# A four-layer attention and expert kernel: TensorE's slots regrouped, the sort cut in three, indirect writes paced anew

## The chip, the cores and the metric

The kernel runs on one core of a Trainium2 chip (trn2). The metric is the device time of one execution in microseconds, lower is better. The kernel before took 880.13 us (median of three runs, 880.06 to 884.29).

## What is computed

The input x has 8 sequences of 256 tokens with 128 channels. Four layers follow one another, each on a normalised x and added to it:

```python
x = x + attn_a(layernorm(x))   # "rope": 16 heads of 8 channels, rotated q, k, v, softmax, rotated back
x = x + ffn(layernorm(x))      # "ffn": h = x + attention(ln1(x)); h + experts(ln2(h))
x = x + attn_b(layernorm(x))   # "cov": centred q, k, plus a product of their variances, softmax
x = x + ffn(layernorm(x))
```

The experts of an ffn layer: every token picks the 2 best of 8 by a gate, each expert is gelu(t @ w1 + b1) @ w2 + b2 with 512 hidden channels, and the two results are mixed with normalised gate weights. All arithmetic is float32 (matrix products of the projections and scores use a float32 form that is split into a rounded and a remaining part).

## The kernel before

**Phases.** There are two phases (`ph`), each with two attention layers (rope and ffn, then cov and ffn) and one expert stage (`mixture`). Every engine has its own instruction stream, written out by hand with semaphores (`need`, `wait_ge`, `then_inc`).

**Attention as a pipeline.** A step s works on up to six blocks (a block is one sequence of 256 tokens) at different stages, named u, t, a, m, n, p from oldest to youngest. In each engine's `step(u, t, a, m, n, p)`, p is normalised (`norm`, GpSimd), n is turned, projected and its q and k stacked and turned (`do_zT`, `do_proj`, `do_kT`, `do_qT`), m has its raw scores taken for the maxima (`do_raw` on TensorE, `do_max` on VectorE), a has its scores, exponentials and products with the values (`do_scores`, `do_exp` on ScalarE, `do_pv`), t is divided, turned and projected out (`do_outT`, `divide`, `do_onT`, `do_wo`, `residual`), and u goes through second normalisation and router (`close` on GpSimd, `do_uT`, `do_gate`, `choose`, `weigh`). There are 16 blocks in a phase, so 16 steps in which `a` exists; a step begins here with the first scores of its `a`.

**TensorE's step (lines 591 to 678).** It has eight slots. Each begins with the scores and raw scores of two heads (32 rows of the array an instruction, lines 444 and 457), goes on to some full-array work (128 by 128), and ends with one `do_pv`: four products of 32 columns each, side by side (line 471), for one key half `kc` of a group `g` of four heads. The two key halves of a group are in slots that follow one another.

**Banks.** PSUM gives four banks to what ScalarE reads (`ring_e`), three to what VectorE reads (`ring_r`: raw scores, projections, outT, gate, wo, rank), one to the products. A bank is taken in order of use, and its next writer waits for the reader of its last content.

**Sort and indirect writes.** In the step with a = block 6 of an ffn layer (`ranking`), the first half's tokens are ranked by expert (`do_rank` on TensorE, `sort_rows` on VectorE, lines 1267 to 1304). `scatter` (line 1554) then issues 16 indirect DMAs on GpSimd's queue that write the rows of U to their sorted places, paced by waits for exponentials (first half) or evacuated expert tiles (second half: `PACE_AT`). A half's sorted rows are loaded only after its 16 writes have landed (`load_x` on SP's queue, line 382).

**Expert stage.** 23 tiles of 128 sorted rows a half: `turn_x`, `hidden`, `outputs` on TensorE (lines 702, 714, 727), gelu on ScalarE, `evacuate` on VectorE (line 1319), then stores, gathers and `combine`. `mixture` begins with the last products of the last block and with `do_weT`, whose copy on ScalarE is a line-833 instruction of WT.

**GpSimd's step (lines 1619 to 1644).** In the order: norm(p) if `early`, close(u), stack_k(n), unrope(t), stack_q(n), stack_v(n), and norm(p) last if not early.

## Time and profile before

| | |
|---|---|
| median of three runs | 880.13 us |
| the profiled execution | 881.32 us |
| its span, first to last instruction | 879.5 us |
| TensorE busy | 780.0 us, 89% |
| VectorE / ScalarE / GpSimd busy | 540.4 / 543.9 / 482.8 us |
| mean granted TensorE clock | 0.926 of full |
| L1114, maxima of raw scores (VectorE) | 326.1 us, 512 instructions |
| L839, exponentials (ScalarE) | 277.0 us, 512 instructions |
| L471, products with the values (TensorE) | 175.8 us, 2048 instructions |

Times are microseconds from the start of the span. PE is TensorE, DVE VectorE, ACT ScalarE, POOL GpSimd. "x8" behind a row is eight instructions merged; the first two numbers are the start and the length of the merged run, which includes the drain of its last instruction, so that the next start tells better how long it held the engine. A bracket is the idle time before and what ended it. PEclk is the granted clock as a share of 2.4 GHz; 0.5 is the lower of the two levels.

### The profile page before, as it was taken

What the parts mean: (1) busy time and instruction counts of PE and PEld (TensorE: products, weight loads), DVE (VectorE), ACT (ScalarE), POOL (GpSimd) and SP (SyncE); (2) the same over time, 40 slices, a digit from 0 to 9 for tenths busy, and PEclk for the clock granted to TensorE, in tenths of its full rate; (3) what the DMA queues carried; (4) which work ended last, traced back from release to release, by engine and by line L of the source; (5) the groups of instructions that cost most, each with busy time, mean ns of one, the idle gap of its engine ahead of it and who ended that gap; (6) DMA issues with size and microseconds to landing.
All of it is one profiled execution on the core that took longest, in us unless ns stands there. A gap on an engine that the chain in (4) does not pass through costs nothing.

```text
span 879.5 us, 21305 instructions
## 1 busy us (share of the span) xinstructions
PE 780.0 (89%) x7166; PEld 552.7 (63%) x7166; DVE 540.4 (61%) x1370; ACT 543.9 (62%) x1264; POOL 482.8 (55%) x906
## 2 busy tenths in 40 slices
PE   1999999999999989987988999999999998998970
PEld 1755655656555459986964555666665544897960
DVE  4699998788878423112486888888887852221232
ACT  0377776877776527544556766787786652764630
POOL 6667777747672550514745765734776344142436
PEclk9999998999998759999999999999999975899995
DMA  9400000000000325765310000000000023465842
GB/s 272 119 3 3 3 3 1 3 3 2 3 3 2 101 70 143 203 182 164 88 37 13 18 17 5 4 2 3 2 3 2 3 63 96 119 199 174 239 118 69
DMA packets 57657, 56.29 MB, mean 64 GB/s; under 512 B 6856, under 2 KB 42448, under 8 KB 57552
## 3 DMA queue, kind: packets, MB, share of 16 engines
q1 hardware_dynamic: 39200, 39.13, 15.8%
q0 software_dynamic: 4096, 8.40, 3.2%
q10 hardware_dynamic: 14256, 7.41, 2.9%
q8 instruction: 61, 1.00, 0.5%
q14 instruction: 44, 0.36, 0.1%
HBM read 40.10 MB, written 14.29 MB: 62 GB/s over the span
## 4 chain that ended last, share of the span: by engine, by line
PE 56%; DVE 22%; POOL 7%; issue 6%; DMA 4%; another core or an unknown queue 2%; ACT 2%; ACTq 0%; POOLq 0%; SPq 0%; DVEq 0%
DVE M L1114 11%; PE bankO L471 10%; PE bankE L714 8%; PE bankR L727 7%; PE bankE L490 7%; PE bankE L444 7%; PE bankR L457 3%; POOL Yg L1590 3%; PE bankE L481 2%; PE bankR L511 2%; DVE QKV L1076 2%; DMA Yg<-sorted_y,SLOT 1%; PE bankE L551 1%; PE bankE L702 1%
## 5 line engine op out<-in xcount | busy, mean ns | idle before, releaser
L1114 DVE TENSOR_REDUCE M<-bankR 128x2 f32<-128x512 f32 x512 | 326.1, 683 | 78.1 <-PE bankR L457 75.1
L839 ACT ACTIVATE Pr<-bankE 128x512 f32<-128x512 f32 x512 | 277.0, 594 | 130.9 <-PE bankE L444 123.0
L457 PE MATMUL bankR<-KQ 32*128 32x256 f32 x1024 | 175.7, 341 | 8.3 <-DVE M L1114 4.8
L471 PE MATMUL bankO<-Pr,Vx 128*32 128x256 f32 x2048 | 175.8, 418 | 0.0
L444 PEld LDWEIGHTS bankE<-KQ 32*128 32x128 f32 x1024 | 82.1, 195 | 102.6 <-issue 73.4
L444 PE MATMUL bankE<-KQ 32*128 32x256 f32 x1024 | 136.8, 344 | 0.0
L457 PEld LDWEIGHTS bankR<-KQ 32*128 32x128 f32 x1024 | 113.1, 192 | 22.0 <-DVE M L1114 17.3
L1572 POOL DMA_INDIRECT sorted_u<-U,SLOT x64 | 62.3, 973 | 100.0 <-DVE Yb L1319 58.0
L956 ACT ACTIVATE G<-bankE,W 128x128 f32<-128x128 f32 x368 | 101.0, 381 | 25.6 <-PE bankE L714 14.6
L1319 DVE COPY Yb<-bankR 128x128 f32<-128x128 f32 x92 | 26.1, 289 | 145.3 <-PE bankR L727 126.0
L714 PE MATMUL bankE<-XTT,W 128*128 128x128 f32 x736 | 102.1, 285 | 4.4 <-ACT G L956 1.4
L1590 POOL DMA_INDIRECT Yg<-sorted_y,SLOT x64 | 62.0, 969 | 73.7 <-DMA sorted_y<-Yb 31.2
L727 PE MATMUL bankR<-w,G 128*128 x736 | 98.1, 278 | 2.3 <-DVE Yb L1319 1.9
L714 PEld LDWEIGHTS bankE<-XTT,W 128*128 128x128 f32 x736 | 93.0, 199 | 7.8 <-issue 4.2
L727 PEld LDWEIGHTS bankR<-w,G 128*128 128x128 f32 x736 | 89.4, 192 | 4.1 <-issue 3.2
L833 ACT ACTIVATE KQ<-bankE 128x512 fp32r<-128x512 f32 x128 | 70.5, 604 | 23.4 <-PE bankE L490 22.9
L471 PEld LDWEIGHTS bankO<-Pr,Vx 128*32 128x32 f32 x2048 | 42.0, 112 | 36.2 <-issue 14.3
L1481 POOL CAST Kst<-QKV 128x512 fp32r<-128x512 f32 x24 | 15.7, 653 | 65.4 <-DVE QKV L1076 39.2
L1406 POOL TENSOR_SCALAR lnsmall<-meanvar 128x2 f32<-128x2 f32 x48 | 11.1, 230 | 70.2 <-DVE meanvar L1044 67.3
L490 PE MATMUL bankE<-ident_r,Zhl 128*128 128x256 f32 (+1 forms) x128 | 24.1, 315 | 23.0 <-POOL X L1452 13.4
L947 ACT ACTIVATE XTT<-bankE,lncols 128x512 f32<-128x512 f32 (+1 forms) x24 | 18.3, 763 | 41.6 <-PE bankE L702 41.6
L490 PE MATMUL bankE<-ident_r,Kst 128*128 128x256 f32 (+1 forms) x256 | 39.2, 299 | 4.1 <-POOL Kst L1484 4.1
(169 smaller groups left out, 1147.7 us busy)
## 6 DMA issues: line engine op xcount, KB each, us to landing
W<-in_w1b SPq DMA_DIRECT2D x92, 258.0 KB
sorted_y<-Yb ACTq DMA_DIRECT2D x92, 64.0 KB
XT<-sorted_u SPq DMA_DIRECT2D x20, 256.0 KB
sorted_u<-Yg SPq DMA_DIRECT2D x2, 1472.0 KB, 9.6
KQ<-MT SPq DMA_DIRECT2D x128, 4.0 KB
X<-in_x SPq DMA_DIRECT2D x8, 128.0 KB, 7.7
sorted_u<-U,SLOT POOLq DMA_INDIRECT x64
Yg<-sorted_y,SLOT POOLq DMA_INDIRECT x64
```

Source lines behind the costliest of these rows:

```text
L444: k = mm(act_bank("S", layer, b, h)[:, z * T:z * T + T], KT[rows, kb, g, z * P:z * P + P], QT[rows, kb, g, :], start=True, stop=True)
L457: k = mm(dve_bank("raw", layer, b, h)[:, z * T:z * T + T], QT[rows, kb, g, z * P:z * P + P], KT[rows, kb, g, :], start=True, stop=True)
L471: k = mm(bankO[SL * j:SL * j + SL, cols], Vx[:, b % VB, kc, HG * g + j, :], Pr[:, g % 2, j, kc, :], start=(g % 2 == 0 and kc == 0), stop=( ...
L490: return mm(bank[:, i * P:i * P + n], src, ident_r[:, 0:n], start=True, stop=True)
L714: k = mm(act_bank("hid", ph, at)[:, c * P:c * P + P], W1[:, n % NW, c * P:c * P + P], XTT[:, (ph * NGRP + q) % 2, j, :], start=True, stop= ...
L727: k = mm(dve_bank("out", ph, at)[:, 0:D], G[:, (ph * NAT + at) % NGB, c, :], w2[:, bass.ds(e * FC + c, 1), :].rearrange("p o d -> p (o d)" ...
L833: return nc.scalar.activation(dst, src, ACT.Copy)
L839: nc.scalar.activation(Pr[:, (h // HG) % 2, h % HG], act_bank("S", layer, b, h).rearrange("p (k q) -> p k q", k=TT), ACT.Exp, scale=EXP_SC ...
L956: nc.scalar.activation(G[:, n % NGB, c, :], act_bank("hid", ph, at)[:, c * P:c * P + P], ACT.Gelu_apprx_tanh, bias=W1[:, n % NW, FF + c:FF ...
L1114: v.tensor_reduce(M[:, b % 2, :, h], dve_bank("raw", layer, b, h).rearrange("p (t k) -> p t k", t=TT), AX.X, ALU.max, negate=True).then_in ...
L1572: g.indirect_dma_start(sorted_u[half][:, :], bass.IndirectOffsetOnAxis(ap=SLOT[:, half, n:n + 1], axis=0), U[:, b, t, :], None).then_inc(s ...
L1590: g.indirect_dma_start(Yg[:, n % NYG], None, sorted_y[half][:, :], bass.IndirectOffsetOnAxis(ap=SLOT[:, half, at:at + 1], axis=0)).then_in ...
```

## The change

TensorE's step keeps its eight slots. Both key halves of a group of heads now stand behind one another in every second slot, and all full-array work stands in the slots between. The next block's `do_zT` moves, for rope and ffn layers, to the end of the step before; it waits for one GpSimd instruction less. `do_kT` stands in the sixth slot and `do_qT` in the eighth for all layers; `do_uT` and the second part of `do_rank` move from the third to the fourth slot, `do_gate` from the fifth to the sixth. ScalarE and VectorE follow the new order. GpSimd normalises p first in every step whose p belongs to a rope or ffn layer. `sort_rows` becomes three functions, called in three places of the step. `do_gate` and `choose` on VectorE move behind the norm statistics of the next block. The first half's indirect writes wait at numbers 3, 9 and 12 only, six instead of five are issued in the sort's step, and the second half's wait for tiles two earlier.

```diff
--- before.py
+++ after.py
@@ -248,6 +248,7 @@
         ffn_only = {"ffn": 1}
         ln_stats = event("ln_stats", 4)
         z_ready = event("z_ready", {"rope": 9, "ffn": 15, "cov": 8})
+        Z_READY = {"rope": 8, "ffn": 14, "cov": 8}
         zT = event("zT", 1)
         zT_copied = event("zT_copied", 1)
         proj = event("proj", 2)
@@ -323,7 +324,8 @@
         STEPS = 2 * NB + 5
         FILL, DRAIN = 3, 2
-        EARLY, PACE_AT = 5, 7
+        EARLY, PACE_AT = 6, 5
+        PACE = {3: (NB - 2, 14), 9: (NB - 1, 10), 12: (NB - 1, 16)}
         def block_of(u):
@@ -341,6 +343,10 @@
             q = max(q for q, (first, _) in enumerate(GROUP) if first <= at)
             return q, at - GROUP[q][0]
+        def turned_ahead(q):
+            return LAYERS[q[0]] != "cov"
         def own_steps(ph):
@@ -490,7 +496,7 @@
                 return mm(bank[:, i * P:i * P + n], src, ident_r[:, 0:n], start=True, stop=True)
             def do_zT(layer, b):
-                need(pe, z_ready, layer, b)
+                need(pe, z_ready, layer, b, Z_READY[LAYERS[layer]])
                 ring_e.take(pe, ("zT", layer, b))
                 for x in range(2):
                     for t in range(TT):
@@ -589,13 +595,15 @@
                 ring_r.give(("fold",), folded, 0, 0)
             def step(u, t, a, m, n, p):
                 if a:
                     do_scores(*a, 0)
                     do_raw(*a, 7)
-                if n:
+                if n and not turned_ahead(n):
                     do_zT(*n)
                 if t:
                     do_pv(*t, 3, 0)
+                    do_pv(*t, 3, 1)
                 if a:
                     do_scores(*a, 1)
@@ -605,8 +613,6 @@
                     do_mT(*a, 1)
                 if ranking(a):
                     do_rank(a[0] // 2, 0, 0)
-                if t:
-                    do_pv(*t, 3, 1)
                 if n:
                     do_proj(*n)
@@ -614,12 +620,9 @@
                     do_scores(*a, 2)
                 if m:
                     do_raw(*m, 1)
-                if ranking(a):
-                    do_rank(a[0] // 2, 0, 1)
-                if u:
-                    do_uT(*u)
                 if a:
                     do_pv(*a, 0, 0)
+                    do_pv(*a, 0, 1)
                 if a:
                     do_scores(*a, 3)
@@ -629,53 +632,50 @@
                     do_outT(*t)
                 if m == (0, 0):
                     do_fold()
-                if a:
-                    do_pv(*a, 0, 1)
+                if u:
+                    do_uT(*u)
+                if ranking(a):
+                    do_rank(a[0] // 2, 0, 1)
                 if a:
                     do_scores(*a, 4)
                 if m:
                     do_raw(*m, 3)
-                if u:
-                    do_gate(*u)
                 if a:
                     do_pv(*a, 1, 0)
+                    do_pv(*a, 1, 1)
                 if a:
                     do_scores(*a, 5)
                 if m:
                     do_raw(*m, 4)
-                if n and LAYERS[n[0]] != "rope":
+                if n:
                     do_kT(*n)
-                if a:
-                    do_pv(*a, 1, 1)
+                if u:
+                    do_gate(*u)
                 if m:
                     do_mT(*m, 0)
+                if t:
+                    do_onT(*t)
                 if a:
                     do_scores(*a, 6)
                 if m:
                     do_raw(*m, 5)
-                if t:
-                    do_onT(*t)
-                if n:
-                    if LAYERS[n[0]] == "rope":
-                        do_kT(*n)
-                    else:
-                        do_qT(*n)
                 if a:
                     do_pv(*a, 2, 0)
+                    do_pv(*a, 2, 1)
                 if a:
                     do_scores(*a, 7)
                 if m:
                     do_raw(*m, 6)
+                if n:
+                    do_qT(*n)
                 if t:
                     do_wo(*t)
-                if n and LAYERS[n[0]] == "rope":
-                    do_qT(*n)
-                if a:
-                    do_pv(*a, 2, 1)
+                if p and turned_ahead(p):
+                    do_zT(*p)
             def do_rank(ph, half, part):
@@ -888,42 +888,38 @@
             def step(u, t, a, m, n, p):
                 if a:
                     do_exp(*a, 0)
-                if n:
+                if n and not turned_ahead(n):
                     do_zT(*n)
+                if t:
+                    do_pv(*t, 1)
                 if a:
                     do_exp(*a, 1)
                     do_mT(*a, 1)
-                if t:
-                    do_pv(*t, 1)
-                if a:
                     do_exp(*a, 2)
+                    do_exp(*a, 3)
                 if u:
                     do_uT(*u)
                 if a:
-                    do_exp(*a, 3)
                     do_exp(*a, 4)
                     do_exp(*a, 5)
-                if n and LAYERS[n[0]] != "rope":
+                if n:
                     do_kT(*n)
                 if a:
                     do_pv(*a, 0)
                 if m:
                     do_mT(*m, 0)
+                if t:
+                    do_onT(*t)
                 if a:
                     do_exp(*a, 6)
                 if block_of(u) is not None:
                     do_gate_exp(*block_of(u))
-                if t:
-                    do_onT(*t)
+                if a:
+                    do_exp(*a, 7)
                 if n:
-                    if LAYERS[n[0]] == "rope":
-                        do_kT(*n)
-                    else:
-                        do_qT(*n)
-                if a:
-                    do_exp(*a, 7)
-                if n and LAYERS[n[0]] == "rope":
                     do_qT(*n)
+                if p and turned_ahead(p):
+                    do_zT(*p)
             def do_gate_exp(ph, j):
                 need(act, gated, ph, j, GAPS)
@@ -1172,8 +1168,6 @@
                     do_proj(*n)
                 if m:
                     do_max(*m, 1)
-                if ranking(a):
-                    sort_rows(a[0] // 2, 0)
                 if n:
                     turn(*n, 0)
                 if rope:
@@ -1187,23 +1181,29 @@
                     divide(*t)
                 if m == (0, 0):
                     do_fold()
+                if ranking(a):
+                    count_tiles(a[0] // 2, 0)
                 if m:
                     do_max(*m, 3)
                 if rope:
                     rotate(*n, 0, 0)
-                if u:
-                    do_gate(*u)
+                if ranking(a):
+                    place_rows(a[0] // 2, 0)
                 if m:
                     do_max(*m, 4)
-                if block_of(u) is not None:
-                    choose(*block_of(u))
                 if rope:
                     rotate(*n, 0, 1)
+                if ranking(a):
+                    name_experts(a[0] // 2, 0)
                 if late(p):
                     combine(0, p[1])
                     norm_in(*p)
                 if nxt and not late(nxt):
                     norm_in(*nxt)
+                if u:
+                    do_gate(*u)
+                if block_of(u) is not None:
+                    choose(*block_of(u))
                 if m:
                     do_max(*m, 5)
                 if rope:
@@ -1264,8 +1264,7 @@
                 need(dve, ranked, ph, half, 1)
                 v.tensor_copy(totals[:], dve_bank("totals", ph, half)[:, 0:P]).then_inc(sorted_.sem, 1)
-            def sort_rows(ph, half):
+            def count_tiles(ph, half):
                 bank = dve_bank("rank", ph, half)
@@ -1285,6 +1284,14 @@
                 v.tensor_reduce(last[:], upto_n[:], AX.X, ALU.add).then_inc(sorted_.sem, 1)
                 done(5)
                 tt(first[:], last[:], ntiles[:, 1], ALU.subtract).then_inc(sorted_.sem, 1)
+            def place_rows(ph, half):
+                bank = dve_bank("rank", ph, half)
+                def done(x):
+                    need(dve, sorted_, ph, half, x)
                 done(6)
                 v.scalar_tensor_tensor(rank[:], first[:].unsqueeze(1).broadcast_to([P, GROUPS, E]), float(P),
                                        bank[:, 0:P].rearrange("p (g e) -> p g e", e=E), ALU.mult,
@@ -1296,6 +1303,12 @@
                 v.tensor_reduce(place[:], rank[:], AX.X, ALU.add).then_inc(sorted_.sem, 1)
                 done(9)
                 v.tensor_copy(SLOT[:, half], place[:]).then_inc(sorted_.sem, 1)
+            def name_experts(ph, half):
+                def done(x):
+                    need(dve, sorted_, ph, half, x)
                 tt(past[:], tile_no.unsqueeze(2).broadcast_to([P, NTL, E]),
                    last[:].unsqueeze(1).broadcast_to([P, NTL, E]), ALU.is_ge).then_inc(sorted_.sem, 1)
                 done(11)
@@ -1342,7 +1355,9 @@
                 if i == 4:
                     copy_totals(ph, 1)
                 if i == 5:
-                    sort_rows(ph, 1)
+                    count_tiles(ph, 1)
+                    place_rows(ph, 1)
+                    name_experts(ph, 1)
                 if i in (15, 19):
                     add_b2(ph, (i - 3) // 4 - 1)
@@ -1564,10 +1579,8 @@
                 for n in part:
                     if half:
                         need(pool, evacuated, ph, PACE_AT + 4 * n // 5)
-                    elif n < EARLY:
-                        need(pool, exped, layer, NB - 2, H - 2 * EARLY + 2 * n + 2)
-                    elif n < 2 * EARLY:
-                        need(pool, exped, layer, NB - 1, 3 * (n - EARLY) + 1)
+                    elif n in PACE:
+                        need(pool, exped, layer, *PACE[n])
                     b, t = divmod(half * HB * TT + n // 2, TT)
                     g.indirect_dma_start(sorted_u[half][:, :],
                                          bass.IndirectOffsetOnAxis(ap=SLOT[:, half, n:n + 1], axis=0),
@@ -1617,7 +1630,7 @@
                 pool.wait_ge(ready_pool, 8)
             def step(u, t, a, m, n, p):
-                early = (t and LAYERS[t[0]] == "rope") or (n and LAYERS[n[0]] == "rope") or (3, 0) in (n, p)
+                early = p and turned_ahead(p)
                 if early and p:
                     norm(*p)
                 fetched = p and p[0] == 2 and 0 < p[1] < NB - 1
```

## Rows read from the trace of the kernel before

**Rows 1.** The page's busy time, share of the span and instructions of each engine
```profile
PE 780.0 (89%) x7166; PEld 552.7 (63%) x7166; DVE 540.4 (61%) x1370; ACT 543.9 (62%) x1264; POOL 482.8 (55%) x906
```

**Rows 2.** Stretches of one step each: length, busy time by engine, clock, DMA
```profile
core 0: us, PE busy (x) PEld busy (x) DVE busy (x) ACT busy (x) POOL busy (x), PEclk, DMA share, GB/s
...
73.40:90.70 17.30, 16.41 (x172) 10.13 (x168) 16.28 (x33) 12.78 (x27) 13.89 (x25) 1.00 0.01 2
...
174.60:190.10 15.50, 15.31 (x172) 9.54 (x168) 12.74 (x27) 12.52 (x26) 8.99 (x18) 1.00 0.01 4
...
222.40:239.10 16.70, 16.22 (x178) 10.15 (x174) 14.30 (x45) 12.79 (x28) 12.18 (x28) 1.00 0.01 4
...
273.60:292.00 18.40, 17.17 (x162) 9.68 (x158) 14.52 (x45) 9.85 (x21) 7.07 (x11) 0.81 0.04 14
...
489.80:507.90 18.10, 16.49 (x175) 10.23 (x171) 15.38 (x33) 12.85 (x26) 11.91 (x23) 1.00 0.07 17
507.90:527.40 19.50, 17.90 (x175) 10.84 (x171) 15.38 (x33) 12.81 (x26) 11.90 (x23) 0.91 0.05 15
```

**Rows 3.** TensorE in order of time in a plain step: start, length, instruction
```profile
175.97 0.64 PE L471 MATMUL bankO<-Pr,Vx 128*32 128x256 f32 x8
...
176.53 0.39 PE L444 MATMUL bankE<-KQ 32*128 32x256 f32 x2
...
176.98 0.38 PE L481 MATMUL bankE<-ident,M 128*8 128x128 f32 x2
...
177.30 0.64 PE L471 MATMUL bankO<-Pr,Vx 128*32 128x256 f32 x8
```

**Rows 4.** TensorE in order of time, at half clock, end of attention
```profile
308.49 1.08 PE L471 MATMUL bankO<-Pr,Vx 128*32 128x256 f32 x8
309.50 0.80 PE L444 MATMUL bankE<-KQ 32*128 32x256 f32 x4
...
311.39 1.94 PE L471 MATMUL bankO<-Pr,Vx 128*32 128x256 f32 x16
313.25 1.02 PE L737 MATMUL bankE<-ident,WE 128*8 128x128 f32 x4
```

**Rows 5.** TensorE in order of time, where two full-array blocks follow one another
```profile
277.13 0.38 PE L481 MATMUL bankE<-ident,M 128*8 128x128 f32 x2
277.35 0.39 PE L686 MATMUL bankR<-sortc,OH 128*128 128x128 f32 x2
```

**Rows 6.** Waits in the plain step 174.6 to 190.1: total, times, longest
```profile
ACT Pr L839 <- PE bankE L444: 2.9, 5, 1.0
DVE M L1114 <- PE bankR L457: 2.4, 3, 1.1
```

**Rows 7.** GpSimd in order of time, first and last instruction of one norm(p)
```profile
231.17 0.23 POOL L1406 TENSOR_SCALAR lnsmall<-meanvar 128x2 f32<-128x2 f32 x1
...
237.49 0.73 POOL L1452 TENSOR_TENSOR Hs<-Y,b_o_ffn 128x256 f32<-128x256 f32 x1
```

**Rows 8.** VectorE in order of time, first and last instruction of the sort
```profile
281.07 0.17 DVE L1278 TENSOR_SCALAR ntiles<-bankR 128x8 f32<-128x8 f32 x1 [0.22 <-PE bankR L694]
...
284.00 0.18 DVE L1304 TENSOR_SCALAR EID<-npast 128x23 uint32<-128x23 f32 x1
```

**Rows 9.** GpSimd, ScalarE and TensorE in order of time, end of attention
```profile
308.85 0.96 POOL L1572 DMA_INDIRECT sorted_u<-U,SLOT  x1 [2.99 <-ACT Pr L839]
...
316.43 0.95 POOL L1572 DMA_INDIRECT sorted_u<-U,SLOT  x1 [0.30 <-issue]
...
318.89 0.59 ACT L833 ACTIVATE WT<-bankE 8x512 f32<-8x512 f32 x1 [7.47 <-remote]
...
319.80 1.11 PE L541 MATMUL bankR<-ident,OT 128*128 128x128 f32 x4 [3.95 <-ACT OT L833]
```

**Rows 10.** GpSimd and TensorE in order of time, turn of the two halves
```profile
377.20 0.95 POOL L1572 DMA_INDIRECT sorted_u<-U,SLOT  x1 [1.26 <-DVE Yb L1319]
...
382.33 1.48 PE L702 MATMUL bankE<-ident,XT 128*128 128x128 f32 x8 [2.44 <-DMA XT<-sorted_u]
```

2 lines of the change are left out of this document (1 added, 1 removed).

## The prediction

> **What bounds the kernel now.** I read the page's busy table first [rows 1]: TensorE is busy 89% of the span, VectorE and ScalarE about 61% each. An average over unlike stages settles nothing, so the table by stretches comes next [rows 2]. Its rows are single steps of the attention pipeline; 32 steps, 16 in each phase, cover some 550 of the 879.5 us. In a plain ffn step (the row at 174.6) TensorE is busy 15.31 of 15.5 us, VectorE 12.74 and ScalarE 12.52: TensorE sets the pace, with little room above the other two. In ffn steps that also carry a finished block's router work (row 222.4; call them loaded) it is 16.22 of 16.7 against 14.30. In rope steps (row 73.4) VectorE has 16.28 of 17.3, so both engines are near the end. Cov steps (row 489.8) take 18.1 with neither full. There the waits form a loop: combine and statistics on VectorE, normalising on GpSimd, turning and projecting on TensorE, back to VectorE.
>
> Busy is not useful, so I then read TensorE's order inside one plain step [rows 3]. A group of eight product instructions (four product matrices of two passes) occupies 175.97 to 176.53, 0.56 us. A block of scores and raw scores takes 0.45 (176.53 to 176.98), and the little transpose after it 0.32. Adding all blocks of this step at such lengths (8 score blocks 3.6, 8 product groups 4.5, full-array work 6.1) gives 14.2, so about 1.3 of the 15.5 are waits for banks or data. The step's waits show who idles in return: ScalarE waits 2.9 us for scores and VectorE 2.4 for raw scores [rows 6].
>
> Three places outside the steady steps matter. The step in which the first half is sorted takes 18.4 us at a clock of 0.81 [rows 2], though it has no next block to prepare; in it VectorE does the sort in one piece, 281.07 to 284.18 [rows 8]. At the end of attention, seven indirect writes follow one another 1.26 us apart. ScalarE sits 7.47 us before a copy, and TensorE 3.95 behind it [rows 9], although the transposes that this copy reads were issued at 313.25 [rows 4]. At the turn of the two halves of the expert stage TensorE waits 2.44 us for the load that must follow the second half's last indirect write [rows 10]. Phase 1 repeats these places with nearly the same lengths.
>
> **The change, part by part.**
>
> *Products in pairs.* The two groups of eight that belong to one bank of heads wait for the same exponentials, so the second adds no wait of its own. What is saved has one witness, at half clock: one group costs 308.49 to 309.50, 1.01 us, and the only back-to-back pair 311.39 to 313.25, 1.86 [rows 4]. So 0.85 us is streaming for each group and 0.16 is paid once per run. At full clock streaming is 0.43, and 0.56 minus 0.43 leaves 0.13. Four pairs a step save 0.5 us. The bounds are 0 and 0.16 a pair; I take 0.13, since the two clocks agree.
>
> *Full-array work together.* A lone transpose costs 0.32 [rows 3]; followed by another full-array block it costs 277.13 to 277.35, 0.22 [rows 5]. That is 0.10 a merge. After the change the projection (after a mT), the other mT and onT (after kT), the output projection and the next block's zT (after qT) follow other full-array work. This is five merges in a plain step, less the one that is split (onT and qT), so 0.4; a loaded step gains two more (uT, gate), 0.6. If a merge saved only half of that, the term is 0.2 to 0.3. The Trainium skill (TensorEngine Tiling (Array Packing), Key Properties) says that only a switch of tiling mode drains the array. By it, a merge within one mode would save all that a switch costs, nearer 0.2 than 0.1, and the sum would gain another 10 us. The trace has 0.10 for the merge it shows, and the sum goes by that.
>
> *What of this reaches the end.* TensorE's content of a plain step falls from 14.2 to 13.3, of a loaded one by 1.1. But VectorE needs 12.74 and ScalarE 12.52, and the raw scores have three banks. I laid the eight slots out with the lengths above and 0.6 us a reduction. The fourth slot's second raw score then waits some 0.4 us for its bank, and the seventh slot's second score some 0.4 for the copies of K. The step comes out at 14.2 to 14.6, that is 0.9 to 1.3 less. GpSimd's new order adds a risk. norm(p), 7.0 us (231.17 to 238.22, [rows 7]), now stands ahead of close(u) and stack_k. Its statistics come late in the step before, so K should be stacked about when kT, now in slot 5, asks for it, and U about when uT does. Behind these two waits stand all later scores, and behind those ScalarE and VectorE. In plain steps GpSimd has 6.5 us of idle time to absorb this, in loaded ones 4.5 (12.18 busy of 16.7). I take 0.9 for each of the 16 ffn steps without a sort: **14.4 us**, bounds 6 and 21.
>
> *Rope and cov.* Rope steps are already at VectorE's length (16.28 of 17.3): 0 for the six, bounds a gain of 3 and a loss of 2, as kT moves one slot ahead while its stack still waits for VectorE's rotations. In cov steps only the piece between Z-turn and projection lies on the loop; it loses one transition and part of a pair, 0.3 a step: **1.8 us** for six, bounds 0 and 5.
>
> *Sort in three pieces, router work later.* The 3.1 us of small operations [rows 8] are spread behind three maxima, so raw scores are no longer held for all of it; rank's matmuls move one slot back, and choose behind the next norm's statistics. ScalarE's gate exponential waits for choose, with the last exponentials behind it; the last raw scores hide this in a steady step. The sort step lost about 4 us: a plain step's 15.5 less the next block's projection and turns (3.9 by their lengths), plus router and rank work (2.7), is 14.3, and it took 18.4. I count 2 us for each: **4 us**, bounds 0 and 8, the clock included.
>
> *First half's writes in threes.* Twelve of sixteen go out while TensorE still has scores, and the last four at the last exponential. At 1.26 us each these end 5.0 us after it instead of the 6.0 (311.4 to 317.4) [rows 9]. I read the 7.47 us as TensorE's results being reported late while the writes run back to back: the wait begins in the seven-write run and ends after it. Four instead of seven leave at most about 5. I take 1.2 us here and 1.0 for pairs and merges in the last attention step, which runs at half clock: 2.2 in each phase, **4.4 us**, bounds 0 and 10.
>
> *Second half's writes two tiles earlier.* The last one moves from 377.20 to about 373.5, so the load starts as much earlier, more than TensorE's whole wait of 2.44 [rows 10]. What is late next is ScalarE's copy of the turned rows, as now. **4.9 us** in both phases, bounds 2 and 5.
>
> Z_READY, one GpSimd addition less ahead of the turn, and the earlier zT cost nothing: in ffn and rope steps norm(p) starts a step ahead of its use.
>
> The sum is 14.4 + 1.8 + 4.0 + 4.4 + 4.9 = 29.5 us. The profiled execution took 881.3 us (span 879.5), 1.2 above the median of 880.13; the median goes to 880.1 - 29.5 = **850.6 us**.
>
> **The rivals.**
> *A, evacuation takes over.* TensorE's savings turn into its own waits, because VectorE and ScalarE cannot empty banks faster. For it: 12.74 and 12.52 of 15.5 [rows 2], and only three raw banks. Against: VectorE still waits 2.4 us a step [rows 6]. The ffn term shrinks to a third, 5 us, and the sum to some 19: 861 us; with late K stacks as well, 870. The Trainium skill (the same page, Performance Considerations) warns that tiling speeds up TensorE but not the emptying of PSUM; this mechanism is that warning at work.
> *B, everything is hidden.* No new waits, the upper bounds of the steps: 21 for ffn, 3 rope, 3 cov, 6 sort, 8 and 5 for the expert stage: 46 us, 834 us.
> *C, the bursts hurt.* If three writes back to back already delay TensorE's reports by 2 us, five bursts in each phase cost up to 20 us: 870. Against: between 308.85 and 311.4 three writes had gone out and no engine waited unusually. It also holds the case that the change does not do what it says, by pacing writes into the very waits it should avoid.
> *D, the clock (slower).* TensorE gets idle pieces in each step and falls to half clock more often. The price is in two like cov steps: 18.1 us at clock 1.00, 19.5 at 0.91 [rows 2], 1.4 us a drop. One drop in each of 30 steps costs 42: 893 us; it decides from 21 such steps on. Against: a cov step had TensorE busy 16.49 of 18.1, 91%, at clock 1.00, about the share I expect after the change (13.3 of 14.6).
>
> **How the numbers follow.** Forecast (842 to 859) 0.47; A 0.27; B 0.11; C 0.07; D 0.08. The range takes the forecast, most of A and half of B: 834 to 872. A measurement tells 0.5%, 4.4 us, from no change. Faster 0.88, with all of the forecast and B and nearly all of A and C; same 0.05, from the ends of A, C and D; slower 0.07, from D.
>
> **What would show it.** Product groups appear as runs of sixteen, about 1.0 us each; a plain step takes 14.2 to 14.8 and a loaded one 15.4 to 16, with VectorE's busy time per step unchanged and its wait for raw scores smaller. PE idle before L490 for Kst, or before uT, of more than 0.5 us a step means A. ScalarE's wait before WT should fall from 7.5 to 5 or less; longer waits in the middle of attention near L1572 mean C. The wait for XT at the half turn should be gone. Clock digits below 9 in more than a third of the attention slices mean D. The prediction is wrong if plain ffn steps stay above 15.2, or if the stretches of the expert stage move by more than 6 us a phase.

## The result and the profile after

The changed kernel takes 849.44 us (median of 4 runs, 846.55 to 853.75) against 881.76 us for the kernel before in the same session. The ratio is 0.9635, 95% interval 0.9584 to 0.9686. The forecast was 850.6 us, with a range of 834 to 872. Ratios leave out runs of more than 1.5% above the fastest of their kernel; the profiled run with Q in the seventh slot, below, is one of them, and its steps are read at clock 1.00 alone.

The profiled run took 846.55 us, the fastest of its four, with a span of 844.7 us, 34.8 less than the 879.5 of before. By the medians the gain is 32.3 us. The page's busy table of the changed kernel (busy time, share, instructions) answers to [rows 1]:

```profile
PE 747.0 (88%) x7166; PEld 556.4 (66%) x7166; DVE 539.7 (64%) x1370; ACT 536.0 (63%) x1264; POOL 484.5 (57%) x906
```

The instructions are the same in number. VectorE's and GpSimd's work is unchanged, TensorE is busy for 33 us less, and its share of the span is a point lower. The gain is TensorE's. The stretches of single steps, then the last attention step with the expert stage of each phase (columns as in [rows 2]):

```profile
75.10:91.50 16.40, 14.85 (x169) 9.62 (x168) 15.55 (x33) 12.39 (x26) 14.01 (x24) 1.00 0.01 2
171.50:186.70 15.20, 15.10 (x172) 9.94 (x171) 12.82 (x27) 12.14 (x27) 11.39 (x25) 1.00 0.01 2
217.20:232.60 15.40, 15.20 (x178) 10.62 (x177) 14.59 (x51) 12.78 (x29) 12.34 (x29) 1.00 0.02 4
263.00:279.90 16.90, 15.11 (x159) 9.65 (x158) 14.09 (x44) 10.98 (x24) 6.15 (x10) 0.90 0.04 11
279.90:432.30 152.40, 138.85 (x1077) 120.71 (x1078) 50.71 (x185) 83.24 (x242) 72.49 (x110) 0.90 0.50 140
470.10:489.00 18.90, 16.23 (x170) 10.65 (x170) 15.30 (x32) 12.46 (x27) 11.99 (x23) 1.00 0.07 17
680.90:844.70 163.80, 125.92 (x995) 110.59 (x994) 41.32 (x165) 77.69 (x232) 67.37 (x82) 0.83 0.51 144
```

and the two expert stages of the kernel before, of which [rows 2] shows only the steps ahead of them:

```profile
292.00:452.50 160.50, 142.84 (x1080) 123.07 (x1078) 50.31 (x185) 82.90 (x243) 71.27 (x109) 0.88 0.47 133
714.40:879.50 165.10, 125.12 (x998) 110.27 (x994) 39.98 (x164) 76.43 (x230) 66.19 (x81) 0.83 0.50 142
```

Measured from one step's first scores to the next step's (a plain step of after begins at 171.46 and the next at 186.69, 15.23 us), the 34.8 us divide so:

| steps | before | after | gain | forecast |
|---|---|---|---|---|
| filling the pipeline and first block | 57.2 | 59.0 | -1.8 | 0 |
| five rope steps (one at clock 0.82 before) | 86.7 | 82.0 | 4.7 | 0 |
| seven plain ffn steps, 15.5 each before | 108.6 | 106.6 | 2.0 | 6.3 |
| eight loaded ffn steps, 16.7 to 19.0 before | 137.1 | 122.2 | 14.9 | 7.2 |
| six cov steps | 111.7 | 110.7 | 1.0 | 1.8 |
| two sort steps | 37.3 | 32.7 | 4.6 | 4.0 |
| two expert stages, each with the last attention step | 325.7 | 316.3 | 9.4 | 9.3 |

(A step between rope and ffn, 15.2 us in both, is left out; it and the seven plain steps are the forecast's eight, 7.2 us.) The sum is near the 29.5 us of the forecast, but it isn't composed as forecast: plain steps gained a third of their term and loaded steps twice theirs. The clock has a part in it: inside these steps TensorE was at half clock for 37.5 us before and for 13.7 us after.

TensorE inside the plain step shows why (start, length, instruction, in order of time; a block of scores and raw products is L450 and L463):

```profile
171.91 1.07 PE L477 MATMUL bankO<-Pr,Vx 128*32 128x256 f32 x16
172.91 0.39 PE L450 MATMUL bankE<-KQ 32*128 32x256 f32 x2
...
173.42 0.38 PE L487 MATMUL bankE<-ident,M 128*8 128x128 f32 x2
173.56 0.42 PE L517 MATMUL bankR<-w_hi_ffn,ZT 128*128 128x384 f32 x1
...
177.21 0.66 PE L547 MATMUL bankR<-ident,OT 128*128 128x128 f32 x4
177.80 0.50 PE L450 MATMUL bankE<-KQ 32*128 32x256 f32 x4
178.13 1.09 PE L463 MATMUL bankR<-KQ 32*128 32x256 f32 x4
179.15 1.07 PE L477 MATMUL bankO<-Pr,Vx 128*32 128x256 f32 x16
```

The pair of product groups holds the engine 1.00 us (171.91 to 172.91) where two groups apart held it 0.57 each (0.56 in the prediction). The turn of the maxima, followed by the projection, holds it 0.14 (173.42 to 173.56) where it held 0.32 [rows 3]. But the block in the fifth slot, 177.80 to 179.15, takes 1.35 where 0.45 would do. "Busy" hides this: the four raw products are one run of 1.09 us, and the page counts it as work. VectorE over the same stretch, in order of time, with idle time and its releaser in the bracket:

```profile
175.66 1.28 DVE L1110 TENSOR_REDUCE M<-bankR 128x2 f32<-128x512 f32 x2
177.38 1.29 DVE L1110 TENSOR_REDUCE M<-bankR 128x2 f32<-128x512 f32 x2 [0.44 <-PE bankR L463]
178.59 0.35 DVE L1120 RECIPROCAL rden<-bankR 128x32 f32<-128x32 f32 x1
178.97 0.49 DVE L1124 TENSOR_TENSOR On<-bankR,rden 128x128 f32<-128x128 f32 x2
```

VectorE first waits 0.44 us for raw products, then needs 1.2 us for the two; the three banks hold these two and the turned output, so TensorE in turn waits in the fifth slot. Each engine waits for the other once in the same step.

### The profile page after: what moved, and what is told of

It reads as the page before. It is cut to its first block, busy times and chain, and to the rows that moved or that the text cites. A ratio compares the mean times of both kernels' runs of the same rounds, so it can differ in the third digit from the quotient of the medians.

```text
span 844.7 us, 21303 instructions
## 1 busy us (share of the span) xinstructions
PE 747.0 (88%) x7166; PEld 556.4 (66%) x7166; DVE 539.7 (64%) x1370; ACT 536.0 (63%) x1264; POOL 484.5 (57%) x906
## 3 DMA queue, kind: packets, MB, share of 16 engines
q1 hardware_dynamic: 39200, 39.13, 16.7%
## 4 chain that ended last, share of the span: by engine, by line
PE 52%; DVE 18%; POOL 15%; issue 8%; DMA 5%; another core or an unknown queue 1%; ACT 1%; SPq 0%; POOLq 0%; ACTq 0%; DVEq 0%
DVE M L1110 10%; PE bankO L477 9%; PE bankE L714 8%; PE bankR L727 8%; PE bankE L450 7%; PE bankE L496 6%; PE bankR L463 3%; POOL Yg L1603 2%; PE bankE L702 1%; PE bankE L487 1%; PE bankR L517 1%; POOL Z L1432 1%; POOL R L1479 1%; POOL Zhl L1462 1%; POOL lnsmall L1423 1%
## 5 line engine op out<-in xcount | busy, mean ns | idle before, releaser
L463 PE MATMUL bankR<-KQ 32*128 32x256 f32 x1024 | 170.6, 339 | 18.0 <-DVE M L1110 8.9
L477 PE MATMUL bankO<-Pr,Vx 128*32 128x256 f32 x2048 | 148.2, 409 | 0.7 <-ACT OT L833 0.7
L450 PE MATMUL bankE<-KQ 32*128 32x256 f32 x1024 | 144.2, 341 | 0.0
L450 PEld LDWEIGHTS bankE<-KQ 32*128 32x128 f32 x1024 | 88.6, 193 | 80.8 <-issue 50.6
L463 PEld LDWEIGHTS bankR<-KQ 32*128 32x128 f32 x1024 | 105.2, 191 | 36.7 <-DVE M L1110 29.6
L952 ACT ACTIVATE G<-bankE,W 128x128 f32<-128x128 f32 x368 | 101.3, 380 | 29.5 <-PE bankE L714 15.3
L1585 POOL DMA_INDIRECT sorted_u<-U,SLOT x64 | 62.5, 976 | 96.7 <-DVE past L1312 41.9
L1603 POOL DMA_INDIRECT Yg<-sorted_y,SLOT x64 | 62.2, 972 | 75.5 <-DVE Yb L1332 32.1
L477 PEld LDWEIGHTS bankO<-Pr,Vx 128*32 128x32 f32 x2048 | 55.4, 113 | 44.4 <-issue 7.8
L943 ACT ACTIVATE XTT<-bankE,lncols 128x512 f32<-128x512 f32 (+1 forms) x24 | 18.4, 765 | 45.7 <-PE bankE L702 34.0
L1343 DVE SCALAR_TENSOR_TENSOR X<-Yg,SH,X 128x128 f32<-128x128 f32 x64 | 22.3, 363 | 29.1 <-DMA Yg<-sorted_y,SLOT 24.8
L496 PE MATMUL bankE<-ident_r,Qst 128*128 128x256 f32 (+1 forms) x256 | 38.3, 294 | 2.6 <-POOL Qst L1519 2.6
```

The lines of the kernel that those rows point to most:

```text
L450: k = mm(act_bank("S", layer, b, h)[:, z * T:z * T + T], KT[rows, kb, g, z * P:z * P + P], QT[rows, kb, g, :], start=True, stop=True)
L463: k = mm(dve_bank("raw", layer, b, h)[:, z * T:z * T + T], QT[rows, kb, g, z * P:z * P + P], KT[rows, kb, g, :], start=True, stop=True)
L477: k = mm(bankO[SL * j:SL * j + SL, cols], Vx[:, b % VB, kc, HG * g + j, :], Pr[:, g % 2, j, kc, :], start=(g % 2 == 0 and kc == 0), stop=( ...
L496: return mm(bank[:, i * P:i * P + n], src, ident_r[:, 0:n], start=True, stop=True)
L952: nc.scalar.activation(G[:, n % NGB, c, :], act_bank("hid", ph, at)[:, c * P:c * P + P], ACT.Gelu_apprx_tanh, bias=W1[:, n % NW, FF + c:FF ...
L1585: g.indirect_dma_start(sorted_u[half][:, :], bass.IndirectOffsetOnAxis(ap=SLOT[:, half, n:n + 1], axis=0), U[:, b, t, :], None).then_inc(s ...
```

## The experiments

All lengths of plain steps below are at a granted clock of 1.00. "Interval" is the time between two blocks of scores and raw products, filled by products and full-array work.

### Pairs alone

```diff
                 if t:
                     do_pv(*t, 3, 0)
+                    do_pv(*t, 3, 1)
...
-                if t:
-                    do_pv(*t, 3, 1)
```

and likewise for groups 0, 1 and 2 of `a`; the kernel before otherwise.

> The kernel before with one edit: both key halves of a group of heads stand behind one another, where the first of them stood; all else is in its old place. Theory (TensorE's regrouping carries most of the gain of some 32 us, and pairs are half of it): runs of sixteen take 1.00 us instead of two times 0.57, the loaded ffn steps fall from 16.73 to about 16.0, the plain ones from 15.5 to 15.3, and the whole is 6 to 10 us faster than before (about 872 to 876). Rival (the pairs' saving is taken back by waits for banks, and the gain comes from the merged full-array work): the whole moves by less than 3 us and the waits of TensorE for raw-score banks grow by what the pairs save. Second rival (pairs leave gaps in which the clock falls): slower than before, with more stretches below 1.00 in the attention part.

Measured: 907.23 us (904.4 to 917.38), ratio 1.036, interval 1.0283 to 1.0437: slower. A plain step and a loaded one with a drop of the clock:

```profile
173.30:189.80 16.50, 16.15 (x171) 10.62 (x170) 12.63 (x27) 12.26 (x27) 9.01 (x17) 1.00 0.01 3
206.30:224.90 18.60, 18.01 (x177) 12.21 (x176) 13.48 (x32) 13.22 (x29) 12.23 (x28) 0.91 0.01 2
```

The plain step grew from 15.5 to 16.5 us although every pair took the 1.00 us that it should. VectorE, in order of time:

```profile
186.76 0.68 DVE L1110 TENSOR_REDUCE M<-bankR 128x2 f32<-128x512 f32 x1
189.31 1.29 DVE L1110 TENSOR_REDUCE M<-bankR 128x2 f32<-128x512 f32 x2 [1.86 <-PE bankR L457]
190.51 0.41 DVE L1131 TENSOR_TENSOR X<-bankR,X 128x256 f32<-128x256 f32 x1
```

and TensorE's first slot of the next step:

```profile
189.78 0.51 PE L444 MATMUL bankE<-KQ 32*128 32x256 f32 x4
190.06 1.09 PE L457 MATMUL bankR<-KQ 32*128 32x256 f32 x4
```

The seventh slot of this kernel has the turns of out and of Q and then the whole pair, 2.5 us between two blocks, so VectorE runs dry for 1.86 us. The eighth has only the output projection, 0.64 us, and TensorE then waits in the first slot. The pairs took 0.56 us out of the products of a step and put 1.4 us into waits.

### The old turn of z, and then Q too

The changed kernel with z turned at the start of its own step and GpSimd's old order:

```diff
             def turned_ahead(q):
-                return LAYERS[q[0]] != "cov"
+                return False
...
-                early = p and turned_ahead(p)
+                early = (t and LAYERS[t[0]] == "rope") or (n and LAYERS[n[0]] == "rope") or (3, 0) in (n, p)
```

> The changed kernel with the turn of z back at the start of the block's own step on TensorE and ScalarE, and with GpSimd's old rule for when it normalizes early. The pairs, the other places of full-array work, sort and writes stay as changed. Theory: the pairs took the cover from TensorE's first slot (in the run of pairs alone its scores and raw products took 1.30 us instead of 0.45 us, waiting for a bank of raw products), and what restores it is the turn of z (0.6 us) put between the output product and the next step's first slot. Then the first slot takes 1.1 to 1.3 us again, plain and loaded steps of the ffn layers grow from 15.2 us to 15.9 to 16.2 us, the rope steps by about as much, and the whole is 865 to 880 us. Rival: the gain of the turn lies only in one mode switch less per step (0.2 us at most): 850 to 855 us. Third: no difference, 848 to 851 us.

Measured: 851.42 us (849.55 to 854.67), ratio 0.968, interval 0.9641 to 0.9719. Plain steps 15.43 us, loaded 15.43 to 15.66. That is the rival: the turn of z is worth 0.2 us in a plain step, nothing that the whole shows. The first slot's block stayed at 0.45 us, so z was not what covered it. The same kernel with one more move undone:

```diff
                 if m:
                     do_raw(*m, 5)
+                if n:
+                    do_qT(*n)
                 if a:
                     do_pv(*a, 2, 0)
                     do_pv(*a, 2, 1)
...
-                if n:
-                    do_qT(*n)
```

> The run with the old turn of z, with one move more undone: the turns of Q stand again in TensorE's seventh slot, ahead of the product group, instead of in the eighth; ScalarE's copy of Q again precedes its last exponentials of the step. Theory: the run of pairs alone was slow because two of its slots (the seventh: out and Q turns, then a pair) held everything and the eighth and first almost nothing, so that VectorE, which needs 1.2 us for each pair of raw products, was idle for 1.9 us and then late, and the first slot took 1.30 us. Then putting Q back alone takes the plain step from 15.43 us to 16.2 to 16.5 us, with the first slot's products at 1.2 to 1.3 us, drops of the clock come with it, and the whole is 870 to 900 us. Rival: the slow steps of the run of pairs alone came from somewhere else (the merges, uT and gate): plain steps stay at 15.4 to 15.7 us and the whole at 850 to 858 us.

Measured: 879.43 us (872.96 to 886.36), ratio 1.0216, interval 1.0121 to 1.0311, against 0.9657 (0.9601 to 0.9713) for the changed kernel on the same chip (below). A plain step:

```profile
197.10:213.60 16.50, 16.23 (x169) 10.65 (x168) 12.64 (x27) 12.38 (x28) 8.97 (x18) 1.00 0.01 3
```

and the raw products of the first slot that follows it:

```profile
213.90 1.10 PE L463 MATMUL bankR<-KQ 32*128 32x256 f32 x4
```

It is the step of pairs alone again, 16.53 us from start to start, with the first slot's raw products at 1.10 us and its whole block at 1.30. Moving the turns of Q by one slot costs 1.1 us a plain step and, by the two ratios (0.968 and 1.0216, from two chips), some 5% of the kernel. My theory held: it had 16.2 to 16.5 us and 870 to 900.

### The pairs split again

The changed kernel, its full-array work where the change put it, but the second group of each pair at the end of the next slot, as here and for the other three:

```diff
                 if a:
                     do_pv(*a, 2, 0)
-                    do_pv(*a, 2, 1)
...
                 if p and turned_ahead(p):
                     do_zT(*p)
+                if a:
+                    do_pv(*a, 2, 1)
```

> The changed kernel with the pairs of product groups split again: the second group of each pair stands at the end of the following slot, behind that slot's full-array work; all else as changed. Four more groups stand apart, at 0.57 us against 0.50 us in a pair, and each brings a switch of its own before and behind it. Theory A (the pairs themselves are worth what they cost in the trace): content grows by 0.56 us and waits do not shrink, plain steps 15.7 to 15.9 us, the whole 858 to 868 us. Theory B (what counts is that the steps' waits are covered, and split groups cover as well as before): the added 0.56 us fall into the 1.8 us of waits in the third, fifth and seventh slots, plain steps 15.2 to 15.5 us, the whole 847 to 856 us.

Measured: 875.55 us (875.25 to 883.32), ratio 1.0225, interval 1.0149 to 1.0301. Both theories missed. A plain step, and TensorE in its third slot:

```profile
182.60:199.10 16.50, 15.50 (x172) 9.69 (x168) 12.61 (x26) 12.14 (x27) 11.39 (x25) 1.00 0.01 3
```
```profile
187.58 0.38 PE L450 MATMUL bankE<-KQ 32*128 32x256 f32 x1 [0.56 <-ACT Pr L843]
```

The content grew by only some 0.25 us (intervals 10.1 against 9.87), and the waits by 1.0; in the second phase the step is 16.3. The third slot's scores even wait for ScalarE. So neither half of the regrouping stands by itself: pairs in the old places 16.5 us, new places with split pairs 16.5, both together 15.2, neither 15.5. The eight intervals of a plain step, worked out from TensorE's order of time, with what the blocks of scores take beyond 8 times 0.45:

| kernel | intervals in us | sum | waits | step |
|---|---|---|---|---|
| before | 1.18 2.13 0.57 1.12 0.57 1.96 1.92 1.21 | 10.7 | 1.25 | 15.5 |
| changed | 1.00 1.58 1.00 0.59 1.00 1.72 1.00 1.98 | 9.9 | 1.8 | 15.2 |
| pairs alone | 1.61 1.64 1.00 0.59 1.00 1.29 2.53 0.64 | 10.3 | 2.6 | 16.5 |
| Q in the seventh | 1.61 1.65 1.00 0.59 1.00 1.72 2.05 0.64 | 10.3 | 2.7 | 16.5 |
| pairs split | 0.57 1.93 0.57 1.13 0.57 2.24 0.57 2.56 | 10.1 | 2.7 | 16.5 |

VectorE needs 1.2 us for two raw products and TensorE 0.45 to make them, so an interval of about 0.76 is covered; a shorter one draws on the banks, a much longer one leaves VectorE dry and doesn't pay back. The slow kernels have their longest intervals, over 2 us, beside one of 0.6. The kernel before has long ones too (2.13, 1.96), and my table does not say in numbers why these cost it less. That part is an account of the slow cases and not a rule that was tested on others. What the runs do show is that neither half of the regrouping is faster without the other.

### Half of the maxima

The maxima over 128 of the 256 keys, all else as changed:

```diff
-    dve_bank("raw", layer, b, h).rearrange("p (t k) -> p t k", t=TT),
+    dve_bank("raw", layer, b, h).rearrange("p (t k) -> p t k", t=TT)[:, :, 0:P],
```

> The changed kernel with each row maximum of the raw products taken over the first 128 of the 256 keys only (this leaves out half of the work of the maxima and changes the shifts), so that VectorE's reduction of one head is about half as long (0.69 us becomes some 0.35 to 0.45 us). Nothing else differs. Theory: in the changed kernel a plain step is 15.23 us because TensorE's raw products wait in the second, third, fifth and seventh slots for banks that VectorE has not yet read (0.07, 0.31, 0.91 and 0.48 us over the unhindered 0.45 us). Then plain steps fall to 13.4 to 13.9 us, those four slots take 0.45 to 0.5 us, and the whole is 810 to 830 us. Rival: ScalarE (12.2 us busy) or the scores' banks hold the slots: plain steps stay at 14.8 to 15.3 us and the whole at 840 to 850 us.

Measured: 817.67 us (815.22 to 818.99), ratio 0.930, interval 0.9273 to 0.9327. A plain step, then VectorE and TensorE around its fifth slot, whose block now takes 0.82 us (171.18 to 172.00):

```profile
165.20:179.50 14.30, 14.30 (x169) 9.67 (x168) 8.67 (x27) 12.13 (x27) 11.31 (x25) 1.00 0.01 2
```
```profile
170.76 0.76 DVE L1110 TENSOR_REDUCE M<-bankR 128x2 f32<-128x256 f32 x2 [0.93 <-PE bankR L463]
```
```profile
171.18 0.39 PE L450 MATMUL bankE<-KQ 32*128 32x256 f32 x2
```

VectorE's length is 0.9 us of the plain step (15.23 to 14.34) and, by the two ratios, some 3.5% of the kernel. But with VectorE busy for only 8.67 of 14.3 us, 1.1 us of waits remain, and the step misses the 13.4 to 13.9 that I expected: the fifth slot's block still takes 0.82, the third's 0.69, and the seventh's stays at 0.93. The cause of this last one is another.

### z turned in the fourth slot

```diff
                 if t:
                     do_outT(*t)
...
+                if p and turned_ahead(p):
+                    do_zT(*p)
```

in place of the end of the eighth slot, and the same on ScalarE.

> The changed kernel with the turn of z of the next block moved from TensorE's eighth slot to its fourth, behind the turn of out (ScalarE's copy of it follows the copy of uT). It asks whether full-array work is worth the same wherever it stands. The fifth slot's products take 1.36 us where 0.45 would do, so 0.6 us of cover ahead of it should take them to 0.75 to 0.8 us; the first slot, which then has no work of its own kind between it and the output product, should go from 0.45 us to 0.9 to 1.3 us. Theory (cover is only moved, the sum of maxima and full-array work sets the step): plain steps 15.2 to 15.5 us and the whole 847 to 856 us. Rival (only the fifth slot is short of cover): plain steps 14.6 to 14.8 us and the whole 836 to 842 us. Second rival (the norm on GpSimd is not ready so early and TensorE waits for it): steps over 16 us, 865 us or more.

Measured: 843.73 us (842.27 to 844.71), ratio 0.9587, interval 0.9558 to 0.9616. A plain step:

```profile
541.40:556.20 14.80, 14.78 (x169) 9.71 (x168) 12.85 (x26) 12.20 (x27) 9.56 (x24) 1.00 0.01 3
```

It is 14.81 us against 15.23. The fifth slot's block went from 1.36 to 0.94 and the first stayed at 0.45: cover taken from an interval of 1.98 costs nothing, given to one of 0.59 it is worth 0.4. The rival had the mechanism and came just short of its numbers. Loaded steps moved by -0.1 to +0.3; there uT already fills the fourth slot, which I take for the reason. This is the best ratio of the study, but its interval overlaps those of the changed kernel, so it isn't shown to be faster than that.

### The sixth slot in another order

On top of it, the turns of the maxima and of out ahead of those of K:

```diff
-                if n:
-                    do_kT(*n)
-                if u:
-                    do_gate(*u)
                 if m:
                     do_mT(*m, 0)
                 if t:
                     do_onT(*t)
+                if n:
+                    do_kT(*n)
+                if u:
+                    do_gate(*u)
```

> The run with the turn of z in the fourth slot, with the sixth slot's work in another order: the turns of the maxima and of out ahead of the turns of K on TensorE, the same on ScalarE, and ScalarE's copy of out ahead of the sixth exponentials, where it was idle for 0.8 us. The seventh slot's scores wait (0.93 us where 0.45 would do) for the banks of ScalarE that the two turns of K took, whose copies take 0.5 us each; behind the new order they wait for the two short copies (0.26 us each). Theory: the seventh slot goes to 0.45 to 0.6 us, plain steps from 14.81 to 14.4 to 14.6 us, the whole to 832 to 840 us. Rival (the maxima that the turn needs are not done, VectorE's work sets the step): the sixth slot waits instead, plain steps 14.7 to 14.9 us, the whole 842 to 847 us.

> The changed kernel itself, on the chip of the three others, so that they can be compared with it directly: 847 to 852 us, plain steps 15.23 us. If the run with z turned in the fourth slot (843.7 us) is better than it by its steps, 0.42 us in each of eight plain steps and 0.1 to 0.3 us in rope steps, and not by its chip, this run stands at 0.962 to 0.966 of the kernel before.

Measured on one chip: reordered 830.01 us (826.85 to 837.31), ratio 0.9674, interval 0.9588 to 0.9759; the changed kernel itself 830.09 us (827.48 to 833.33), ratio 0.9657, interval 0.9601 to 0.9713. The kernel before took 860.43 there. I had expected 847 to 852 us of the changed kernel, the time of its first session; its ratio is the one that was expected if z in the fourth slot is better by its steps (0.962 to 0.966). A plain and a loaded step of the reordered kernel, and TensorE in the sixth slot:

```profile
539.70:554.20 14.50, 14.34 (x170) 9.52 (x169) 12.85 (x26) 12.36 (x28) 9.51 (x25) 1.00 0.01 3
597.70:612.80 15.10, 14.84 (x175) 10.26 (x174) 13.52 (x31) 12.81 (x29) 12.37 (x30) 1.00 0.02 5
```
```profile
184.70 0.38 PE L487 MATMUL bankE<-ident,M 128*8 128x128 f32 x2
185.82 0.44 PE L557 MATMUL bankE<-ident,O 128*128 128x128 f32 x2 [0.74 <-POOL O L1554]
186.02 1.13 PE L496 MATMUL bankE<-ident_r,Kst 128*128 128x256 f32 x8
187.08 0.39 PE L450 MATMUL bankE<-KQ 32*128 32x256 f32 x2
```

The seventh slot's block fell to 0.45 us as the theory said: its 0.48 us was the wait for the two banks with K. But the turn of out now waits up to 0.74 us for GpSimd's `unrope` where t is a rope block, which neither theory named. Plain steps reach 14.49 us in the second phase and 15.10 in much of the first. The loaded steps took 61.1 and 61.0 us for four in the changed kernel's run beside it and take 62.5 and 62.2 here, which takes back 2.5 of the 4 us that plain steps gain. The whole gains nothing.

### Writes: in threes alone, paced earlier alone, and undone

The first run adds the new first-half pacing alone to the kernel before, the second the earlier second half alone:

```diff
-        EARLY, PACE_AT = 5, 7
+        EARLY, PACE_AT = 6, 7
+        PACE = {3: (NB - 2, 14), 9: (NB - 1, 10), 12: (NB - 1, 16)}
```
```diff
-        EARLY, PACE_AT = 5, 7
+        EARLY, PACE_AT = 5, 5
```

The third is the changed kernel with the first half's old waits:

```diff
-        EARLY, PACE_AT = 6, 5
-        PACE = {3: (NB - 2, 14), 9: (NB - 1, 10), 12: (NB - 1, 16)}
+        EARLY, PACE_AT = 5, 5
...
-                    elif n in PACE:
-                        need(pool, exped, layer, *PACE[n])
+                    elif n < EARLY:
+                        need(pool, exped, layer, NB - 2, H - 2 * EARLY + 2 * n + 2)
+                    elif n < 2 * EARLY:
+                        need(pool, exped, layer, NB - 1, 3 * (n - EARLY) + 1)
```

> The kernel before with only the first half's indirect writes paced anew (waits at numbers 3, 9 and 12, six in the sort's step). Theory (TensorE's results are reported late while more than three or four writes run back to back): ScalarE's idle time before the copy of WT falls from 7.47 and 7.51 us to below 4, the stretch from the last attention step to the first evacuated tile (42.3 us in both phases) shrinks by 3 us in each phase, the whole by 4 to 7 us (875 to 878). Rival (the wait before WT has nothing to do with the number of writes in a row): the wait stays above 6 us and the whole within 2 us. Rival (moved, not removed): the wait at WT goes, but the six writes of the sort step lengthen it and the next by as much, whole within 2 us.

> The kernel before with only the second half's indirect writes two tiles earlier. Theory (TensorE waits at the turn of the halves for the load behind the last write): the time from tile 22 to tile 23 falls from 10.28 and 10.22 us to about 7.8, the whole by 4 to 5 us (877). Rival (longer rows of writes delay the tiles during the first half by as much): 10.2 falls too, but tiles 0 to 22 (45.65 and 45.37 us) take 1 to 2 us longer, and the whole gains less than 3 us.

> The changed kernel with the old pacing of the first half's indirect writes (one write each time, five held before the last step); all else, the second half's earlier pacing too, is left as changed. Theory: the writes in threes are what took ScalarE's wait for the w_e turns at the end of attention from 7.5 us to 2.1 us, as the change's run of threes alone on the kernel before also lost that wait while the run with only the earlier second-half pacing kept it at 7.5 us. Then the wait of some 7 us comes back in both phases, the stretch from the start of the last attention step to the next block of attention grows from 152.5 us by 3 to 5 us, and the whole is 852 to 859 us. Rival: the earlier start of the second half's writes did the work and the threes add nothing: 848 to 851 us. A second rival: the six writes that the change issues back to back in the sort step cost those steps, so undoing them gains: the sort steps (16.8 and 15.8 us) lose 1 us each and the whole is 845 to 848 us.

Measured: threes 873.18 us (869.42 to 878.92), ratio 0.9946, interval 0.9916 to 0.9975; earlier second half 874.57 us (871.9 to 877.72), ratio 0.995, interval 0.9919 to 0.9982; old waits in the changed kernel 853.78 us (852.78 to 855.9), ratio 0.971, interval 0.9679 to 0.9742. ScalarE's first copy of WT, phase 0, in the threes alone, the earlier second half, the old waits and the changed kernel, in this order:

```profile
312.54 0.59 ACT L834 ACTIVATE WT<-bankE 8x512 f32<-8x512 f32 x1 [2.46 <-issue]
```
```profile
313.93 0.59 ACT L833 ACTIVATE WT<-bankE 8x512 f32<-8x512 f32 x1 [6.29 <-remote]
```
```profile
303.13 0.59 ACT L832 ACTIVATE WT<-bankE 8x512 f32<-8x512 f32 x1 [4.39 <-PE bankE L736]
```
```profile
303.05 0.59 ACT L833 ACTIVATE WT<-bankE 8x512 f32<-8x512 f32 x1 [2.12 <-PE bankE L737]
```

With the writes in threes this wait is 2.46 us (2.92 in the second phase) where it was 7.47 and 7.51 [rows 9]. The second half's pacing doesn't touch it: 6.29 and 7.51. Undone in the changed kernel, the threes bring back 4.39 and not the 7 that I expected, so up to 3 us of it went with other parts, the order of TensorE's work among them. The whole is 4 us above the changed kernel, as expected, but the two were timed in different sessions, and the ratios' intervals (0.9679 to 0.9742, 0.9584 to 0.9686) overlap: what the threes are worth inside the changed kernel isn't shown. On the kernel before, in one session of ten runs each, either pacing is worth half a per cent.

How they bring it is less clear than the theories had it. The stretch from the last attention step to the first evacuated tile, 42.3 and 42.4 us before, is 35.7 and 36.8 with the threes, but also 36.1 and 43.8 with the earlier second half, which changes nothing there; the long ones are at a granted clock of 0.64 and 0.65, the short ones at 0.71 to 0.81. So the length of this stretch goes with the clock, and these traces can't say what the threes give there. And the time from tile 22 to tile 23, which the earlier second half should take from 10.3 to 7.8 us, is 9.9 and 7.6, while tiles 0 to 22 take 0.6 and 0.9 us longer.

### The sort in three pieces alone

The three pieces with their places, and rank's second part one slot later, in the kernel before:

```diff
-                if ranking(a):
-                    sort_rows(a[0] // 2, 0)
...
+                if ranking(a):
+                    count_tiles(a[0] // 2, 0)
                 if m:
                     do_max(*m, 3)
...
+                if ranking(a):
+                    place_rows(a[0] // 2, 0)
...
+                if ranking(a):
+                    name_experts(a[0] // 2, 0)
```

> The kernel before with the sort in three pieces behind three maxima, and the second part of rank in the fourth slot of TensorE's step. Theory (the sort holds raw scores back): the two sort steps (18.41 and 18.91 us) fall by about 2 us each, the whole by 4 (877 to 878). Rival (the sort step's length comes from the late reports while indirect writes run, and from half clock): the two steps stay within 0.7 us and the whole within 2 us.

Measured: 880.95 us (876.57 to 885.25), ratio 1.0018, interval 0.9993 to 1.0044. The first sort step of this kernel, and the same step with the uncut sort in the run of the second half's pacing:

```profile
272.80:294.30 21.50, 18.76 (x163) 10.25 (x159) 16.01 (x48) 10.91 (x22) 7.25 (x11) 0.68 0.04 12
```
```profile
272.70:293.90 21.20, 19.87 (x160) 10.61 (x156) 16.56 (x50) 11.03 (x22) 7.71 (x12) 0.68 0.05 15
```

At the same clock it takes about the same time, cut or uncut, 0.3 us more if anything. The second sort step can't be compared so: it took 23.07 us with 17.7 us at half clock, against 19.02 with 10.2. The cut alone gains nothing.

## Why the prediction came out

**The total: part luck.** The median fell by 32.3 us against 29.5, by errors that cancelled. Of the 34.8 us between the two traces, plain steps brought 4.3 less than forecast and loaded steps 7.7 more; rope steps and the filling, both put at nothing, brought 4.7 and -1.8. The clock, which the sum had only as a risk, helped: 23.9 us less at half clock inside the steps. At the prices seen below (1.24 us for a record of 3.4, 1.9 for one of 6.8) that is an estimated 7 to 9 of the 34.8 us. How much of it belongs to the change isn't shown: the changed kernel's second trace has 30.7 us at half clock in the same steps, and three more traces of TensorE's old order have 41, 41 and 66. And both things that I had said would make the prediction wrong happened: plain steps stayed above 15.2 us, by 0.03, and the first expert stage's stretch moved by 8.1 us, where 6 was the limit.

**Products in pairs: right in price.** 0.14 us a pair by the trace, 0.13 forecast. But "the second adds no wait of its own" was the wrong question. Alone the pairs cost 3.6%: they empty one interval and overfill another, and moving the turns of Q alone switches that loss on and off.

**Full-array work together: right in sign, too small.** The turn before the projection fell by 0.18, against 0.10 a merge. The Trainium skill (TensorEngine Tiling (Array Packing), Key Properties) has the drain at a switch of tiling mode alone. This turn stood between instructions of other shapes before and is followed by a full-array one now, and its 0.18 agrees with the larger price. The content of a plain step went from 14.26 to 13.5 us (13.3 forecast).

**What reaches the end: this step of the prediction failed,** and with it the term of 0.9 us a step. I laid out the slots and found 0.4 us of waits in the fourth and 0.4 in the seventh, a step of 14.2 to 14.6. The trace has 0.31, 0.91 and 0.48 in the third, fifth and seventh, 1.8 in all where before had 1.25, and a step of 15.23, just past the 15.2 at which I had said the prediction would be wrong. The waits for K and U that I feared from GpSimd's new order did not come: K's turns start at the end of the sixth slot's block and take 0.99 us, uT 0.31. The seventh slot's was foreseen with its cause, which the reordered run showed. The fifth I had one slot early and half as large: the layout let VectorE work without a pause, while it first waits 0.44 us for raw products and then has them late. So in plain steps rival A came true to its third (2.0 of 6.3 us); halving the maxima took 0.9 us off the step, 0.7 of it from the waits, so VectorE holds at least that much, and the turns of K hold 0.48.

**Loaded steps made up for it.** I gave them 0.9 us and they gained 1.9 on average, 1.7 without the drop of the clock named below. In the changed kernel uT and gate stand in the fourth and sixth slots, ahead of the two blocks that wait anyway: those fall to 1.14 and 0.71 us in the step at 201.9, and a loaded step ends as short as a plain one, 15.23. Before, they stood in product slots with a switch on both sides. My account of merges counted 0.2 us for this; that they would fill waits was missing. Beyond a plain step a loaded one had 0.96 us more in its intervals and 0.2 more in waits before; now it has 0.3 more in intervals and 0.3 less in waits. That the plain step's unfilled fifth slot has room was then used by the turn of z. One more part is the clock: of these eight steps one at 3.4 us of half clock before (18.99 us) shows none after. In the run with the earlier second half the same step, uncut by a drop, takes 17.75, so a drop is 1.24 us here.

**Rope steps: 0 forecast, 4.7 measured,** less 1.8 lost while the pipeline fills. One of the five was at clock 0.82 before, 19.38 us; in the two traces with only the writes paced anew it takes 17.49, so 1.9 of the 4.7 is the drop alone. In the rest VectorE was not as final as its 16.28 of 17.3 made me think: it is busy for 15.55 us of the 16.4 now. No run takes the rope steps apart, so which part of the change did this stays open.

**Sort: right in sum, wrong in cause.** 4.6 us against 4. The pieces alone gained nothing. In the changed order a sort step without a drop takes 15.8 us (five such steps in three runs), and before it took 18.4 and 18.9 with 6.8 us at half clock each. At equal half clock little of the gain is left: the changed kernel's second trace has 6.8 us at half clock in its first sort step and takes 18.02 against 18.41. So most of the gain of that step is the clock, which the term had only included. This is one pair of steps, and no run had the new order with the old sort.

**Expert stages: right in sum, differently made.** The first gained 8.1 us and the second 1.3. The last attention step up to the first evacuated tile gained 3.4 us in one phase and nothing in the other (2.2 each forecast). The turn of the halves gained 1.8 and 2.7 us: the last write comes at 357.96, 39.2 us behind the first evacuated tile (318.74), where it came at 377.20, 42.9 behind it (334.28): 3.7 us earlier, as worked out, but the wait for XT [rows 10] did not go. It fell from 2.44 us in each phase to 1.0 and 1.8. Ahead of the turn, tiles 0 to 22 took 0.5 and 1.2 us longer, so that the earlier writes brought 2.8 us net where 4.9 was forecast. Another 3.5 us came behind it in the first phase, and between two executions of the changed kernel these stretches differ by more than that (below). The terms can't be checked more finely.

**The rivals.** The sums of two were off: A's should be 20 us, not 19, and B's "upper bounds" are 3, 6 and 8 where the terms had 5, 8 and 10. C, the bursts, looks real in this trace: six writes now follow one another in the sort step, and ScalarE waits behind them. GpSimd's first and last of them, then ScalarE:

```profile
276.10 1.23 POOL L1585 DMA_INDIRECT sorted_u<-U,SLOT  x1 [7.63 <-DVE SLOT L1305]
...
282.70 0.96 POOL L1585 DMA_INDIRECT sorted_u<-U,SLOT  x1 [0.30 <-issue]
...
283.50 0.60 ACT L839 ACTIVATE Pr<-bankE 128x512 f32<-128x512 f32 x1 [3.00 <-remote]
```

In the second phase the wait is 3.97 us, and TensorE's first block of the last step takes 2.82 us in the first phase and 5.81 in the second. The later bursts of three show no such wait. Against my reading of the 7.47 us: the copy of WT at 303.05 ran while the four last writes (301.20 to 305.96) were being issued. And the same kernel on chip 4 issues the same six from 279.95 on and ten in a row from 291.09 to 303.57, and ScalarE waits 0.96 us at that place, for TensorE:

```profile
282.85 1.08 ACT L839 ACTIVATE Pr<-bankE 128x512 f32<-128x512 f32 x2 [0.96 <-PE bankE L450]
```

Before WT it waits 1.26 us, and TensorE's first blocks take 0.98 and 0.79. "Remote" stands where the trace names no engine of the core as the releaser. None of the four traces of chip 4 has such a wait; each of the ten others has five or more of over 0.5 us. So a row of writes alone doesn't delay the reports. What differs between the chips or sessions stays open, and with it the cause behind the first half's term. D, the clock, did not come: time at half clock inside the attention steps fell. The run of pairs alone had it, with 3.4 or 6.8 us at half clock in each of its first four loaded steps.

## What to carry over

Where several engines pass banks to one another in one fixed order, a cheaper instruction group can cost more in waits than it saves: list the time between one block of the shared resource and the next, slot by slot, before moving anything, and put work that must be done anyway in front of the block that waits. That uneven intervals are what costs fits the slow kernels here, not the kernel before. A part of a change can be harmful alone and good with the others (pairs alone 3.6% slower, the rest of the change with split pairs 2% slower, all of it 3.6% faster), so parts are to be tried both ways, one added and one undone. "Busy" TensorE time contains waits for banks; only the order of time shows them. A sum that comes out says little of its terms: here two traces of one kernel differ by more than several of them.

## What the hardware showed beyond that

- **The same kernel in another session.** The changed kernel took 849.4 us in one session and 830.1 in another, on chip 4, the kernel before 881.8 and 860.4 (878.4 and 880.3 on chips 5 and 15; the chip of the first session isn't on record). Plain and loaded ffn steps agree to 0.03 us between the two traces; the expert stages don't. Of the second session:

```profile
283.70:430.30 146.60, 128.32 (x1077) 115.91 (x1078) 49.92 (x184) 82.39 (x242) 72.30 (x111) 0.97 0.51 146
679.60:831.50 151.90, 114.97 (x995) 105.58 (x994) 40.43 (x164) 76.43 (x231) 66.23 (x81) 0.88 0.54 155
```

  The first was 152.4 us at a granted clock of 0.90 and is 146.6 at 0.97, the second 163.8 at 0.83 and 151.9 at 0.88. Most of it is the stretch from the last attention step to the first evacuated tile, here in the first phase of the first session and of the second:

```profile
279.88:318.74 38.86, 35.76 (x219) 23.16 (x219) 11.18 (x49) 19.19 (x42) 21.54 (x34) 0.60 0.37 107
283.73:315.97 32.24, 24.99 (x219) 17.27 (x219) 10.14 (x49) 18.26 (x42) 21.48 (x34) 0.89 0.45 129
```

  In the second phase it is 42.5 us at 0.64 against 32.2 at 0.84. The waits ended by "remote" are missing there as well. Only kernels of one session can be compared by their microseconds.
- **A switch of shape costs TensorE more than I took.** A little turn between two blocks of other shape holds the engine 0.32 us; followed by its own kind 0.14.
- **More waits and more drops came together, in these traces.** The kernel of pairs alone has 168 us at half clock, the kernel before 131 (but a second trace of nearly its code, the one with the sort in pieces, has 159). TensorE waits more in it, and its loaded steps go to 18.6 us at clock 0.91 where one without a drop takes 17.9.
